# Two layers with a scan and a mixture of experts: the order of a tile's steps in the first layer, and the PSUM banks they use

## The reference, cut to what matters

```python
x = x + _L0_attn_ref(xn, ...) + _L0_ffn_ref(xn, ...)
# scan branch: for each of 16 state indices n, along the 512 tokens of a sequence
h = exp(delta * A[n]) * h + delta * xn * B[n];   y += h * C[n]      # and y + xn * D
# expert branch: softmax router, 4 of 16 experts for each token
acc += (silu(x @ w_gate.T) * (x @ w_up.T)) @ w_d.T * cw[:, None]    # widths 256 -> 176 -> 256
```

## Time and profile before

| | us |
|---|---|
| median of three runs | 1451.61 (1442.69 to 1452.65) |
| the profiled execution | 1439.03 |
| its span, first to last instruction | 1437.2 |

### The profile page before, as it was taken

How to read it: one execution, slowest core, us unless ns; L and a number is a source line. 1 busy time by engine, 2 the same in 40 slices (tenths; PEclk the granted TensorE clock), 3 DMA queues, 4 the chain that set the end, 5 groups by cost and what they waited for, 6 DMA issues and landing times.

```text
span 1437.2 us, 19673 instructions
## 1 busy us (share of the span) xinstructions
PE 1076.4 (75%) x6400; PEld 629.3 (44%) x6400; DVE 907.6 (63%) x1489; ACT 517.7 (36%) x1131; POOL 469.8 (33%) x366
## 2 busy tenths in 40 slices
PE   2551899967777776777525478799979988999796
PEld 1140455534444443444214245355645654565454
DVE  3678222377877878778862854566566655565685
ACT  2550000044444444444403010544455445344532
POOL 1000100057777777777510330032223322222100
PEclk9855899998998989789856599999989999899998
DMA  9004810056776677767655001354425433443112
GB/s 365 0 0 130 237 24 0 0 134 123 126 141 125 115 133 130 132 122 123 118 127 140 4 16 23 81 129 94 99 63 130 100 88 88 99 95 77 12 49 75
DMA packets 113199, 138.89 MB, mean 97 GB/s; under 512 B 36262, under 2 KB 99350, under 8 KB 112918
## 3 DMA queue, kind: packets, MB, share of 16 engines
q0 software_dynamic: 34976, 77.93, 29.1%
q1 hardware_dynamic: 78134, 59.82, 15.3%
HBM read 70.71 MB, written 37.23 MB: 75 GB/s over the span
## 4 chain that ended last, share of the span: by engine, by line
PE 57%; DVE 19%; ACT 9%; issue 6%; DMA 6%; SPq 2%; ACTq 1%; POOL 0%; DVEq 0%; POOLq 0%
PE bank L412 9%; PE bank L675 8%; PE bank L421 5%; PE bank L692 4%; PE bank L1073 3%; PE bank L1066 3%; PE bank L1394 3%; DVE xnT L807 3%; PE bank L1435 3%; PE bank L1371 2%; DVE cv L1610 2%; PE bank L1384 2%; PE bank L1386 2%; PE bank L1421 2%; ACT yo L749 2%
## 5 line engine op out<-in xcount | busy, mean ns | idle before, releaser
L483 POOL DMA_INDIRECT sum_d<-yo,to_i x128 | 224.7, 1756 | 464.3 <-ACT yo L1093 366.3
L824 POOL DMA_INDIRECT xg<-xn_d,token_i x80 | 105.0, 1313 | 305.7 <-DMA sum_d<-x 142.0
L675 PE MATMUL bank<-areaA,xgT 128*128 x320 | 134.6, 549 | 64.2 <-ACT yo L749 54.4
L807 DVE TENSOR_TENSOR_SCAN xnT<-areaB,xnT 128x1024 f32<-128x1024 f32 x64 | 146.6, 2291 | 4.6
L692 PE MATMUL bank<-areaA,hidT 88*128 x320 | 96.2, 425 | 41.4 <-ACT hidT L742 35.5
L675 PEld LDWEIGHTS bank<-areaA,xgT 128*128 128x128 f32 x320 | 60.4, 210 | 119.5 <-issue 105.2
L1560 DVE TENSOR_TENSOR areaD<-areaD,gb 128x512 f32<-128x512 f32 x128 | 87.7, 689 | 24.6 <-ACT areaD L1521 24.0
L1521 ACT ACTIVATE areaD<-bank 128x512 f32<-128x512 f32 x128 | 76.2, 596 | 63.2 <-PE bank L1386 58.0
L692 PEld LDWEIGHTS bank<-areaA,hidT 88*128 88x128 f32 x320 | 58.4, 203 | 72.5 <-issue 67.3
L412 PE MATMUL bank<-xnT,areaB 128*128 x192 | 84.8, 602 | 1.9 <-issue 1.9
L1394 PE MATMUL bank<-xnT,w_in 128*128 128x512 f32 x160 | 82.2, 641 | 1.5 <-ACT ecn L1280 1.5
(11 more groups left out here) (323 smaller groups left out, 2157.6 us busy)
## 6 DMA issues: line engine op xcount, KB each, us to landing
y<-xnT POOLq DMA_DIRECT2D x64, 512.0 KB, 5.3
wst<-gu_f SPq DMA_DIRECT2D x96, 176.0 KB
wst<-down_f SPq DMA_DIRECT2D x48, 176.0 KB
gu_f<-in_gu POOLq DMA_DIRECT2D x1, 5632.0 KB, 18.4
areaA<-in_gu SPq DMA_DIRECT2D x2, 2816.0 KB
down_f<-in_down POOLq DMA_DIRECT2D x1, 2816.0 KB, 23.6
areaA<-in_down SPq DMA_DIRECT2D x2, 1408.0 KB
sum_d<-yo SPq DMA_DIRECT2D x1, 2176.0 KB, 12.5
```

Of the source, the lines that this page charges most:

```text
L483: nc.gpsimd.indirect_dma_start(sum_d[l], bass.IndirectOffsetOnAxis(ap=to_i[:, q:q + 1], axis=0), yo[:, q % ring, :], None, compute_op=ALU. ...
L675: last = nc.tensor.matmul(bank[:, GB + q % 2, 0:2 * FI], xgT[:, q % 2, k, :], wgu0_of(e, k), start=(k == 0), stop=(k == KD - 1))
L807: nc.vector.tensor_tensor_scan(h, dA[:, u % 2, :], h, 0.0, ALU.mult, ALU.add).then_inc(da_free, 1)
L824: nc.gpsimd.indirect_dma_start(xg[:, q % 5, :], None, xn_d[0], bass.IndirectOffsetOnAxis(ap=token_i[:, q:q + 1], axis=0)).then_inc(s.gathe ...
```

## The change

The down product leaves the gate_up banks and goes to bank HY, which is the old HB and still takes the transposed silu rows. So gate_up no longer waits for a y copy, while the silu transposes wait for the y copy of the tile before. On TensorE the silu transposes go ahead of the row products of their tick, and the x transposes of q+2 go from part 1 to part 2, behind the down product; on ScalarE their copy follows, behind the y copy. The silu of q+1 on VectorE goes from part 1 to part 2. Behind the stage, the transposes of y use banks 4 to 7, and the first eight of the 16 token tiles wait for the additions of their two sequences alone.

```diff
-                self.w_expert, self.experts_done = sem("w_expert0"), sem("experts_done0")
+                self.w_expert = sem("w_expert0")
...
-        BROW, CROW, XB, HB, GB = 0, 2, 4, 5, 6
+        BROW, CROW, XB, HY, GB = 0, 2, 4, 5, 6
...
 def gate_up(pe, q):
             pe.wait_ge(s.xT_ready, q + 1)
-            if q > 1:
-                pe.wait_ge(s.y_ready, q - 1)
...
 def hid_transposes(pe, q):
             pe.wait_ge(s.hid_ready, q + 1)
             if q:
-                pe.wait_ge(s.hT_ready, q)
+                pe.wait_ge(s.y_ready, q)
             for h in range(2):
-                last = nc.tensor.transpose(bank[0:FH, HB, h * P:(h + 1) * P], ...)
+                last = nc.tensor.transpose(bank[0:FH, HY, h * P:(h + 1) * P], ...)
...
 def down(pe, q):
-                last = nc.tensor.matmul(bank[:, GB + q % 2, 0:D], ...)
+                last = nc.tensor.matmul(bank[:, HY, 0:D], ...)
...
 def layer0_tensor(pe):
             for t in range(TICKS0):
+                q, part = divmod(t, TILE)
+                if part == 1 and q < NT0:
+                    hid_transposes(pe, q)
                 pair = (t + 2) // (2 * UNIT)
                 if t % (2 * UNIT) == 2 * UNIT - 2 and pair < UN // 2:
                     b_product(pe, pair)
                 if t and t % (2 * UNIT) == 0:
                     c_product(pe, t // (2 * UNIT))
-                q, part = divmod(t, TILE)
                 if part == 0 and q + 1 < NT0:
                     gate_up(pe, q + 1)
-                if part == 1 and q < NT0:
-                    hid_transposes(pe, q)
-                if part == 1 and q + 2 < NT0:
-                    x_transposes(pe, q + 2)
                 if part == 2 and q < NT0:
                     down(pe, q)
+                if part == 2 and q + 2 < NT0:
+                    x_transposes(pe, q + 2)
...
 def layer0_scalar(act):
                 if part == 1 and q < NT0:
                     hT_copy(act, q)
-                if part == 1 and q + 2 < NT0:
-                    xT_copy(act, q + 2)
                 if part == 2 and q < NT0:
                     y_copy(act, q)
+                if part == 2 and q + 2 < NT0:
+                    xT_copy(act, q + 2)
                 if t % UNIT == 0 and t // UNIT + 1 < UN:
                     decay(act, t // UNIT + 1)
...
 def layer0_vector(v):
-                if part == 1 and q + 1 < NT0:
+                if part == 2 and q + 1 < NT0:
                     silu(v, q + 1)
...
-            nc.vector.sem_inc(s.experts_done, 1)
...
 def scan_out_tensor(pe):
-            pe.wait_ge(s.experts_done, 1)
-            for k in range(4):
-                pe.wait_ge(y_added[k], 16 * (UN // 4))
+            pe.wait_ge(s.y_ready, NT0)
             for t in range(TT):
+                if t % 8 == 0:
+                    for hf in range(2):
+                        pe.wait_ge(y_added[2 * (t // 8) + hf], 16 * (UN // 4))
...
-                    last = nc.tensor.transpose(bank[:, t % 4, hf * P:(hf + 1) * P], ...)
+                    last = nc.tensor.transpose(bank[:, XB + t % 4, hf * P:(hf + 1) * P], ...)
```

More of the change, by code:

```diff
@@ L681, in hid_transposes @@
             if q:
-                pe.wait_ge(s.hT_ready, q)
+                pe.wait_ge(s.y_ready, q)
             for h in range(2):
-                last = nc.tensor.transpose(bank[0:FH, HB, h * P:(h + 1) * P], hid[:, q % 2, h * FH:(h + 1) * FH], ident[:, :])
+                last = nc.tensor.transpose(bank[0:FH, HY, h * P:(h + 1) * P], hid[:, q % 2, h * FH:(h + 1) * FH], ident[:, :])
             last.then_inc(s.hT_full, 1)
@@ L691, in down @@
             for h in range(2):
-                last = nc.tensor.matmul(bank[:, GB + q % 2, 0:D], hidT[:, q % 2, h, :], wd0_of(e, h), start=(h == 0), stop=(h == 1))
+                last = nc.tensor.matmul(bank[:, HY, 0:D], hidT[:, q % 2, h, :], wd0_of(e, h), start=(h == 0), stop=(h == 1))
             last.then_inc(s.y_full, 1)
@@ L741, in hT_copy @@
             act.wait_ge(s.hT_full, q + 1)
-            nc.scalar.activation(hidT[:, q % 2, :, :], bank[0:FH, HB, 0:2 * P].rearrange("p (k t) -> p k t", k=2), ACT.Copy).then_inc(s.hT_ready, 1)
+            nc.scalar.activation(hidT[:, q % 2, :, :], bank[0:FH, HY, 0:2 * P].rearrange("p (k t) -> p k t", k=2), ACT.Copy).then_inc(s.hT_ready, 1)
         def y_copy(act, q):
@@ L748, in y_copy @@
                 act.wait_ge(s.yo_free, q - 4)
-            nc.scalar.activation(yo[:, q % 5, :], bank[:, GB + q % 2, 0:D], ACT.Copy, scale=slot_w[:, q % 5:q % 5 + 1]).then_inc(s.y_ready, 1)
+            nc.scalar.activation(yo[:, q % 5, :], bank[:, HY, 0:D], ACT.Copy, scale=slot_w[:, q % 5:q % 5 + 1]).then_inc(s.y_ready, 1)
         def layer0_scalar(act):
@@ L865, in scan_out_tensor @@
                 for hf in range(2):
-                    last = nc.tensor.transpose(bank[:, t % 4, hf * P:(hf + 1) * P], y[:, hf, t * P:(t + 1) * P], ident[:, :])
+                    last = nc.tensor.transpose(bank[:, XB + t % 4, hf * P:(hf + 1) * P], y[:, hf, t * P:(t + 1) * P], ident[:, :])
                 last.then_inc(yT_full, 1)
@@ L873, in scan_out_vector @@
                     v.wait_ge(x_back[t // 4], 16)
-                nc.vector.tensor_tensor(x0[:, t, :], bank[:, t % 4, 0:D], x0[:, t, :], ALU.add).then_inc(yT_free, 1)
+                nc.vector.tensor_tensor(x0[:, t, :], bank[:, XB + t % 4, 0:D], x0[:, t, :], ALU.add).then_inc(yT_free, 1)
                 if t:
```

## The result

The changed kernel takes 1476.15 us (median of four runs, 1470.15 to 1486.5), beside 1451.21 for the kernel before in the same comparison (1442.69 to 1452.65): ratio 1.0187, interval 1.0142 to 1.0232. That is slower by 1.9%, inside the range and 9 us above the point forecast. The profiled run is the longest of the four, 1486.5 us around a span of 1484.5, so it is read with the clock beside it: over the four runs the mean granted clock of the whole execution is 0.853, 0.856, 0.863 and 0.869, in the order in which they get faster. Runs more than 1.5% above the fastest of their kernel are left out of the ratios (two of four in x_move_silu, three of four in rows_first, whose profiles are of such runs), so there the ratio is not the quotient of the medians.

What follows compares the result with a forecast made beforehand. No engine was full, so a loop of waits was taken to set the stage's pace, gate_up waiting for the y copy. Loop +26, end -4, clock 0, less 2 for the mean load, gave +20 us: 1467 us, range 1442 to 1494.

Steps and rivals of the forecast that it cites:

- the longer wait behind the removed one: Gate_up waits for an x copy queued behind the y copy: +0.71 us a tile, +0.54 with the short load of 0.65.
- The rival in which the load is hidden: ScalarE's register load runs ahead of the waiting y copy: growth only 0.26 us a tile, total 1439; chance 0.10.
- the loop term: Expert stage's loop at full clock: eight tiles go from 38.27 to 40.86 us, +26 us over 80 tiles.
- The small steps: In eight tiles, row products leave the path before the silu transposes, -0.88 us, and the middle decay starts earlier, -0.72.
- rival 1: TensorE's clock suffers from the longer stretch between down and gate_up: +25 us on top, 1492; chance 0.16.
- the forecast case: The slower loop with the stage's clock share unchanged: +20 us, 1467, own range 1452 to 1480; chance 0.52.
- the longest pauses, behind late products, go: Argument against a lower clock: TensorE's pauses of 1.42 and 2.49 us, where 0.72 and 1.70 are the rule, disappear.
- well under 78.6: Sign to look for: VectorE's idle time ahead of silu in the stage falls well below 78.6 us.
- the eight-tile account: Loop sum over eight full-clock tiles; silu one tick later removes the late B and C products' waits, -0.70 and -0.79 us.
- the end: Behind the stage, the first eight token tiles move under VectorE's idle time: -4 us, at most 5.4.
- Rival 4: GpSimd's chain of scatters paces the stage in either order, so only the end gains: -4 us, 1443; chance 0.07.
- the account of the loop closes without GpSimd: Argument against GpSimd's pacing: the loop's listed waits sum to 38.07 us for eight tiles, against 38.27 measured.

Runs made afterwards that it cites:

- x_move_silu: Kernel before with the x transposes and their copy moved to part 2 and silu one tick later, nothing else; median 1529.05 us, ratio 1.0414.
- rows_first: Changed kernel with TensorE's row products put back ahead of the silu transposes of their tick; median 1512.35 us, no ratio given.
- Experiment 3: Changed kernel with ScalarE's register load and slot_w copy put behind the x copy instead of ahead of it; 1442.83 us, ratio 0.9940.
- load_behind: The same run as Experiment 3: changed kernel with register load and slot_w copy behind the x copy; 1442.83 us, ratio 0.9940.
- Filler: Changed kernel with three dummy transposes of a constant behind each pair of x transposes; 1447.73 us, ratio 0.9973.
- silu_back: Changed kernel with silu on VectorE put back to its old tick, part 1; 1498.92 us, ratio 1.0317.
- tail_alone: Kernel before with only the edit behind the stage (y transposes in banks 4 to 7, earlier token tiles); 1447.03 us, ratio 0.9988.
- x_back: Changed kernel with the x transposes and their copy put back to part 1; 1438.66 us, ratio 0.9897.

## Why the prediction was right, and where its steps were off

**Right: the longer wait behind the removed one.** The forecast had gate_up released by the x copy, with 0.64 to 0.82 + 0.11 + 0.50 from the y copy. It came as 0.64 + 0.11 + 0.50, and the plain tile as 4.65 against a forecast 4.66 for the short load. Experiment 3 shows that the register load is its cause: with the load behind the x copy, 0.88 stands between y copy and gate_up, 0.16 over the 0.72 of before, and the tile is 4.28, 0.16 over 4.12. The rival in which the load is hidden, by the row pitch of 0.37, has fallen: slot_w follows the y copy by 0.64 or 0.65 in 54 of 78 tiles, up to 1.27 in the others. The Trainium skill (Advanced Engine Details and Errata, Engine Queue Depths) gives ScalarE a queue 8 deep; behind a copy that waits for TensorE, the trace shows no load hidden by it, in none of the 78 tiles.

**Mis-sized: the loop term, +26 forecast, +15 measured.** Eight tiles were put at 40.86 and took 39.80. The term at fault is the load, put at 0.82 from ScalarE's idle time ahead of slot_w. In these eight tiles it is 0.64 or 0.65 six times, 0.85 and 0.92, which is 0.71 in the mean and takes 0.9 of the 1.06 off; over the stage the mean is 0.77. The small steps, -0.88 for the row products and -0.72 for the decay, held where they can be read: tanh to silu-row copy is 0.21 without a decay, only two of the eight places carry a decay, and rows_first has 5.09 in place of 4.65 in a tile with a product.

**Wrong: the clock, put at 0, +29 in the profiled run.** This was rival 1, given +25 and a chance of 0.16. It came beside the forecast case, not in its place. And the prediction had said that it is wrong if the stage's clock moves by more than 0.05: it moved by 0.08, so by its own sign this part of the mechanism was wrong. The stretch in which TensorE has only the x transposes was named there. Filler fills it and gets 0.10 of clock and 33.6 us of the stage back with the tile unchanged, and load_behind shortens it and gets 0.09, so the clock falls with this pause; whether by its length or by the share of work, is open. The Trainium skill (TensorE: Matmul & The Clock Gate, A second HAM failure mode) says that small pauses between groups of matmuls can make the clock swing; the trace agrees, with 0.91 to 0.83 by the change and 0.93 with filler. The step that failed was the weighing: "the longest pauses, behind late products, go" was held against the rival. They went, and the clock fell all the same; 1.1 us ahead of 75 of 80 gate_ups did more than the few long pauses had.

**Wrong: VectorE's idle ahead of silu, "well under 78.6", measured 122.1.** The silu one tick on takes the wait from VectorE's multiplies, but each step is longer and VectorE's work is the same 322 us, so the idle time of a longer stage must go somewhere. This sign was badly chosen. What the tick gives shows in silu_back. Its loop at full clock is 41.4 us against 39.9, 1.5 more, where the eight-tile account gave 0.70 + 0.79; but two of its eight places rest on one and on two tiles, and the waits of the row products' weight loads came back to 5.1 us only, of 16.6. The stage of the profile is 15.0 longer, and 1.49 in eight tiles is 14.7 over 79 steps, but the clock moved by 0.03 between the two, so this agreement is luck in part.

**Mis-sized: the end, -4 forecast with a bound of -5.4, measured -8.0.** Half the token tiles under VectorE's idle time is 5.4. The rest comes from the last addition itself: TensorE got its rows 8.79 us after issue before (736.37), and 5.57 in tail_alone (738.64 - 733.07). In the kernel before the loads of x are issued 4.5 us ahead of the last addition and in tail_alone 10 us, so they overlap less; that this is why it lands sooner is argued, not tried. The condition named in the forecast, "if x is back from DRAM", decides: in load_behind x is late and the whole gain is gone.

**Not foreseen: the rest of the execution.** It is 10 us longer in the changed kernel's profile, but over the fourteen kernels it lies between 689.8 and 705.3 with no pattern by edit. It is left open; it moves the total as much as the small steps do.

**The sum.** Forecast +20, measured +24.9 in the medians and +47.3 between two profiles that lie apart by chance too. In the profiles the terms are +15 (loop, +26 forecast), +29 (clock, 0), -8 (end, -4) and +11 outside both. The total lay in the range because errors cancel, and that is luck: the loop was put 11 too high and the end 4 too high, the clock at nothing.

**Rival 4 was misjudged in its meaning.** "GpSimd's chain of scatters paces the stage in either order" is wrong for the changed kernel, whose gathers are never waited for. But "the account of the loop closes without GpSimd" was no ground to give the chain room: the four kernels that wait more than 20 us for gathers and don't merge additions run at 5.05 to 5.22 a step, and the kernel before runs at 5.16. With the scatters left out, x_back's order does 4.24.

## What to carry to other kernels

When a wait is taken off an engine's queue, look at what stands between the new releaser and its consumer on the releasing engine's queue, register loads included: here the load took 0.37 of the 0.53 us by which the plain tile grew. A loop that is bound by waits has two prices, the pause itself and the clock that the pause costs, and cheap dummy work in the pause tells them apart. Before a gain is forecast, measure the next floor by leaving its work out: here it lay within 0.1 us of the step that was there.

## What the runs showed of the hardware

- A register load on ScalarE behind a copy that waits for a semaphore started 5 or 6 ns after that copy did, in all 78 tiles. The load took 0.27 to 0.90 us, and the next instruction came 0.64 behind the copy in 54 tiles and up to 1.27 in the others; an x copy in the load's place started 0.37 behind it.
- In a chain of scatters that each wait for the last one's landing, two started 4.37 us apart at the closest (kernel before) and 5.2 in the median (x_back), beside the gathers and additions on the same queue.
- An accumulating DMA of 1 MB lands in 8.5 us where one of 512 KB takes 5.0, and TensorE then waited 142.8 us for gathers in place of 80.4.
- TensorE's clock can stay low for tens of tiles: in rows_first the last 43 tiles of the stage have a mean of 0.72, on the same work as the 36 before them at 0.88. Three dummy transposes a tile held 0.93 where 0.83 was granted.
- Work that no kernel here changed, behind the stage, took 689.8 to 705.4 us.
